# Cross-attention output stage: reciprocals spread in two bursts of four head pairs on 32-row groups of the array

## The reference

```python
qh = (q @ Wq + bq);  kh = (k @ Wk + bk);  vh = (v @ Wv + bv)      # per head, 64 wide
attn = einsum('bqhd,bkhd->hbqk', qh, kh) * mask
attn = exp(attn - max(attn)) * mask                               # one maximum over everything
attn = attn / (sum(attn, axis=-1, keepdims=True) + 1e-15)
out = einsum('hbqk,bkhd->bqhd', attn, vh) @ Wo + bo
x = out + residual
y = (x - mean(x)) / sqrt(var(x) + 1e-05) * gamma + beta
```

## Time and profile before

| | |
|---|---|
| Median of three runs | 1731.38 us |
| The profiled execution | 1729.62 us |
| Its span on the core | 1727.8 us |
| PE busy | 1666.0 us (96%) |
| DVE busy | 1157.9 us (67%) |
| ACT busy | 945.0 us (55%) |
| POOL busy | 419.0 us (24%) |
| Granted TensorE clock, mean | 0.986 |

### The profile page before, as it was taken

One profiled execution on the slowest core, in us unless ns is written; L12 is line 12 of the kernel. 1 busy time (PEld: TensorE's weight loads), 2 busy tenths in 40 slices (PEclk: granted clock), 3 DMA queues, 4 the chain that ended last, 5 costly groups with the idle time before them and its releaser, 6 DMA issues. The chain is left out here.

```text
span 1727.8 us, 31110 instructions
## 1 busy us (share of the span) xinstructions
PE 1666.0 (96%) x11011; PEld 848.1 (49%) x11012; DVE 1157.9 (67%) x2362; ACT 945.0 (55%) x1417; POOL 419.0 (24%) x519
## 2 busy tenths in 40 slices
PE   4999999999999999999995999999999999999997
PEld 4435556465464654645542444444444444444443
DVE  7665555665556655566545887878787877887774
ACT  7755555555545555455544555555564556555542
POOL 0000000000000000000000555555555555555556
PEclk8999999999999999999997999999999999999999
DMA  7455354452644526445236456655655456555621
GB/s 232 147 200 172 119 211 161 161 188 103 225 147 175 188 84 243 140 172 193 74 146 223 159 199 243 231 215 193 234 223 190 190 221 243 218 209 204 243 107 65
DMA packets 81469, 315.01 MB, mean 182 GB/s; under 512 B 5392, under 2 KB 9616, under 8 KB 71696
## 3 DMA queue, kind: packets, MB, share of 16 engines
q1 hardware_dynamic: 81424, 314.41, 49.7%
HBM read 184.37 MB, written 130.02 MB: 182 GB/s over the span
## 5 line engine op out<-in xcount | busy, mean ns | idle before, releaser
L70 PE MATMUL ps_s<-x_hi,g_hi 128*128 128x512 f16 x1024 | 389.7, 381 | 7.5 <-ACT s L509 7.4
L72 PE MATMUL ps_s<-x_hi,g_lo 128*128 128x512 f16 x1024 | 389.3, 380 | 0.0
L71 PE MATMUL ps_s<-x_lo,g_hi 128*128 128x512 f16 x1024 | 389.3, 380 | 0.0
L79 PE MATMUL ps_o<-u,p_hi 128*128 128x512 f16 x1024 | 388.4, 379 | 0.0
L80 PE MATMUL ps_o<-u,p_hi 128*128 128x512 f16 x1024 | 388.1, 379 | 0.0
L81 PE MATMUL ps_o<-u,p_lo 128*128 128x512 f16 x1024 | 388.1, 379 | 0.0
L509 ACT ACTIVATE s<-ps_s,c_bias 128x512 f32<-128x512 f32 x256 | 176.0, 688 | 309.5 <-PE ps_s L72 306.3
L631 DVE TENSOR_TENSOR score_max<-score_max,tile_max 128x1 f32<-128x1 f32 x257 | 40.8, 159 | 315.6 <-ACT s L509 313.8
L898 ACT ACTIVATE p_hi<-ps_bc 128x512 f16<-128x512 f32 x256 | 149.4, 593 | 176.9 <-DVE ps_bc L988 174.9
L1079 POOL PARTITION_ALL_REDUCE key_max<-score_max x1 | 0.4, 377 | 917.0 <-issue 917.0
L1099 POOL TENSOR_TENSOR y<-y,gamma_b 128x512 f32<-128x512 f32 x128 | 162.8, 1272 | 192.6 <-ACT y L908 192.6
(11 more groups left out here) (87 smaller groups left out, 2367.9 us busy)
## 6 DMA issues: line engine op xcount, KB each, us to landing
scores<-s SPq DMA_DIRECT2D x30, 2048.0 KB, 7.6
s<-scores SPq DMA_DIRECT2D x30, 2048.0 KB, 7.8
x<-xT_in SPq DMA_DIRECT2D x32, 1024.0 KB, 9.5
u_halves<-u_out SPq DMA_DIRECT2D x64, 512.0 KB, 3.0
u<-u_halves SPq DMA_DIRECT2D x16, 2048.0 KB, 11.8
y<-x_in SPq DMA_DIRECT2D x32, 1024.0 KB, 10.2
out<-y SPq DMA_DIRECT2D x31, 1024.0 KB, 4.2
mask<-maskT_in SPq DMA_DIRECT2D x32, 256.0 KB, 10.4
```

Source lines behind the costliest of these rows:

```text
L70: pe.matmul(out, lhs_hi, rhs_hi, start=first, stop=False)
L71: pe.matmul(out, lhs_hi, rhs_lo, start=False, stop=False)
L72: return pe.matmul(out, lhs_lo, rhs_hi, start=False, stop=last)
L79: pe.matmul(out, lhs_hi, rhs_hi, start=False, stop=False, skip_group_check=True)
```

## The change

The three product banks and four spread banks (`OBANKS` 3, `RBANKS` 4) trade places. The spreads of a unit come in two bursts, before (0,2) and before (2,0), each of eight matmuls for four pairs. Each matmul uses only the 32 rows of its own q, in weights and data, so that four matmuls in a row use four different row groups and four different banks. Each burst has two rounds of four; between them PE waits on a new semaphore, `r_halves`, which the first round's last matmul raises, since the second round writes the other half of the same banks. The sums move from before (1,7) to directly behind the second burst. Pairs are taken in the order 0, 1, 4, 5, 2, 3, 6, 7, in which both halves of four pairs cover all four q. With three banks for four tiles, the bank of a tile is the running tile number modulo 3, but for the last of a group (`o_bank`), and `fill` waits for the tile 2, 3 or 4 before (`o_since`); the first product tile of a new bank must have been read by `residual`. ACT's fills and DVE's scales, splits and residuals stand in a new order.

```diff
-SBANKS, GBANKS, OBANKS, RBANKS = 2, 4, 4, 3
+SBANKS, GBANKS, OBANKS, RBANKS = 2, 4, 3, 4
...
-        spread_at = {(0, 2): 0, (0, 5): 1, (1, 0): 2, (1, 3): 3, (1, 6): 4, (2, 1): 5, (2, 4): 6, (2, 7): 7}
-        sums_at = (1, 7)
+        spread_at = {(0, 2): 0, (2, 0): 1}
+        sums_at = (2, 0)
+        order = (0, 1, 4, 5, 2, 3, 6, 7)
+        def o_bank(u, t):
+            k = u * TB + t
+            return ps_o[1 if k == UNITS * TB - 1 else k % OBANKS]
+        def o_since(u, t):
+            return {0: 4, 1: 2, 2: 4, UNITS * TB - 1: 2}.get((u * TB + t) % (UNITS * TB), OBANKS)
...
-            def spread(n, s, p):
-                if p == 0:
+            def spread(n, s, half):
+                if half == 0:
                     pe.wait_ge(r_all_done, n + 1)
-                pe.wait_ge(p_lo_done, n * NP + (p + 1 if p >= RBANKS else (2, 3, 1)[p]))
-                for th in range(2):
-                    mm = pe.matmul(ps_bc[p % RBANKS][:, th * HT:(th + 1) * HT], sel_bc[:, p, th, :], r_all[:, s, :],
-                                   start=True, stop=True)
-                mm.then_inc(r_spread, 1)
+                pe.wait_ge(p_lo_done, n * NP + half * RBANKS + RBANKS)
+                for k in range(2):
+                    if k == 1:
+                        pe.wait_ge(r_halves, 2 * n + half + 1)
+                    for j in range(RBANKS):
+                        p, th = order[half * RBANKS + j], (j + k) % 2
+                        q = 2 * th + p // 4
+                        mm = pe.matmul(ps_bc[j][:, th * HT:(th + 1) * HT], sel_bc[32 * q:32 * q + 32, p, th, :],
+                                       r_all[32 * q:32 * q + 32, s, :], start=True, stop=True, skip_group_check=True)
+                    if k == 0:
+                        mm.then_inc(r_halves, 1)
+                mm.then_inc(r_spread, RBANKS)
...
-                    for p in range(NP):
-                        if more and (t, p) in spread_at:
-                            spread(n + 1, 1 - s, spread_at[t, p])
-                        if more2 and (t, p) == sums_at:
+                    for i, p in enumerate(order):
+                        if more and (t, i) in spread_at:
+                            spread(n + 1, 1 - s, spread_at[t, i])
+                        if more2 and (t, i) == sums_at:
                             sums(n + 2, s)
                         if t == 0:
-                            pe.wait_ge(p_lo_done, n * NP + p + 1 + RBANKS)
+                            pe.wait_ge(p_lo_done, n * NP + i + 1 + RBANKS)
                         cols = slice(t * P, (t + 1) * P)
-                        mm = add_product(pe, ps_o[t % OBANKS][:, :], (p_hi[:, s, p, cols], p_lo[:, s, p, cols]),
+                        mm = add_product(pe, o_bank(u, t)[:, :], (p_hi[:, s, p, cols], p_lo[:, s, p, cols]),
                                          (u2[:, b, place(p), 0, :], u2[:, b, place(p), 1, :]))
                     mm.then_inc(o_summed, 1)
...
-            def round_p(n, s, p):
-                if p == 0:
+            def round_p(n, s, i):
+                if i == 0:
                     act.wait_ge(o_summed, TB * n + TB)
-                act.wait_ge(p_scaled, n * NP + p + 1)
-                act.activation(p_hi[:, s, p, :], ps_bc[p % RBANKS][:, :], ACT.Copy).then_inc(p_hi_done, 1)
-            def fill(n, t):
-                act.wait_ge(y_added, n * TB + t + 1)
-                act.activation(ps_o[t % OBANKS][:, :], bo_b[:, :], ACT.Copy, scale=P_SCALE * U_SCALE).then_inc(bo_filled, 1)
+                act.wait_ge(p_scaled, n * NP + i + 1)
+                act.activation(p_hi[:, s, order[i], :], ps_bc[i % RBANKS][:, :], ACT.Copy).then_inc(p_hi_done, 1)
+            def fill(n, u, t):
+                act.wait_ge(y_added, n * TB + t + 1 + TB - o_since(u % UNITS, t))
+                act.activation(o_bank(u % UNITS, t)[:, :], bo_b[:, :], ACT.Copy, scale=P_SCALE * U_SCALE).then_inc(bo_filled, 1)
...
-                    if more:
-                        fill(n + 1, 0)
+                    if u < UNITS - 1:
+                        fill(n, u, 3)
                     norm(g, u, 0)
                     halves(4, 5)
                     if more2:
                         r_first(n + 2)
+                    if u == UNITS - 1:
+                        fill(n, u, 3)
                     if more:
-                        fill(n + 1, 1)
+                        fill(n + 1, u + 1, 0)
                     norm(g, u, 1)
                     halves(6)
                     if more2:
                         r_second(n + 2)
                     halves(7)
+                    if u < UNITS - 1:
+                        fill(n + 1, u + 1, 1)
+                    norm(g, u, 2)
+                    if u == UNITS - 1 and more:
+                        fill(n + 1, u + 1, 1)
                     if more:
-                        fill(n + 1, 2)
-                    norm(g, u, 2)
-                    if more:
-                        fill(n + 1, 3)
+                        fill(n + 1, u + 1, 2)
...
                     split(0)
                     scale(2)
                     split(1)
-                    residual(g, u, 0)
                     scale(3)
                     split(2)
+                    residual(g, u, 0)
+                    split(3)
                     shift_of(g, u, 0)
                     scale(4)
-                    split(3)
+                    scale(5)
+                    residual(g, u, 1)
+                    split(4)
                     if more2:
                         invert(n + 1)
-                    residual(g, u, 1)
-                    scale(5)
-                    split(4)
-                    shift_of(g, u, 1)
                     scale(6)
                     split(5)
+                    shift_of(g, u, 1)
                     if more2:
                         second_part(n + 1)
                     scale(7)
                     split(6)
-                    residual(g, u, 2)
                     if more2:
                         third_part(n + 1, 1 - s)
                     split(7)
+                    residual(g, u, 2)
                     shift_of(g, u, 2)
```

More of the change, by code:

```diff
@@ L726, in output_phase @@
         rest_done, r_mid_done, r_all_done = sem("rest_done"), sem("r_mid_done"), sem("r_all_done")
-        r_spread, p_scaled = sem("r_spread"), sem("p_scaled")
+        r_halves, r_spread, p_scaled = sem("r_halves"), sem("r_spread"), sem("p_scaled")
         p_hi_done, p_lo_done = sem("p_hi_done"), sem("p_lo_done")
@@ L867, in _ @@
             sums(0, 0)
-            for p in range(NP):
-                spread(0, 0, p)
+            for half in range(2):
+                spread(0, 0, half)
             sums(1, 1)
@@ L952, in _ @@
                 round_p(0, 0, p)
-                if p % 2 == 1:
-                    fill(0, p // 2)
+                if p % 2 == 1 and p < 2 * OBANKS:
+                    fill(0, 0, p // 2)
             r_first(1)
@@ L963, in _ @@
             dve.sem_inc(p_lo_done, RBANKS)
-            dve.sem_inc(y_added, OBANKS)
+            dve.sem_inc(y_added, TB)
             def invert(n):
@@ L983, in third_part, with scale_p, split_p @@
                    .then_inc(r_all_done, 1)
[L985 to L992, removed]
+            def scale_p(n, s, i):
+                dve.wait_ge(r_spread, n * NP + i + 1)
+                spread = ps_bc[i % RBANKS][:, :]
+                dve.tensor_tensor(spread, s32[:, s, order[i], :], spread, ALU.mult).then_inc(p_scaled, 1)
+            def split_p(n, s, i):
+                dve.wait_ge(p_hi_done, n * NP + i + 1)
+                p = order[i]
+                dve.tensor_tensor(p_lo[:, s, p, :], ps_bc[i % RBANKS][:, :], p_hi[:, s, p, :], ALU.subtract)\
                    .then_inc(p_lo_done, 1)
@@ L1002, in residual @@
                 y = y32[:, u, t, :]
-                dve.scalar_tensor_tensor(y, ps_o[t % OBANKS][:, :], 1 / (P_SCALE * U_SCALE), y, ALU.mult, ALU.add)\
+                dve.scalar_tensor_tensor(y, o_bank(u, t)[:, :], 1 / (P_SCALE * U_SCALE), y, ALU.mult, ALU.add)\
                    .then_inc(y_added, 1)
-                dve.wait_ge(y_added, k + 1 + OBANKS)
+                dve.wait_ge(y_added, k + 1 + TB)
                 dve.bn_stats(stats[:, t, :], y)
@@ L1063, in _ @@
             third_part(0, 0)
[L1064 to L1068, removed]
+            for half in range(2):
+                for i in range(half * RBANKS, (half + 1) * RBANKS):
+                    scale_p(0, 0, i)
+                    if i % RBANKS > 0:
+                        split_p(0, 0, i - 1)
+                split_p(0, 0, i)
             invert(1)
```

## The result

The changed kernel takes 1759.89 us in the median of four runs (1759.25 to 1760.04), against 1731.66 us for the kernel before (1730.5 to 1732.52). The ratio is 1.0165, 95% interval 1.015 to 1.0179: slower by 1.65%, 28.2 us. The profiled execution takes 1760.04 us with a span of 1758.2, 30.4 more than the span before. That is 2.2 more than between the medians, because the profiled execution of the kernel before lies 2.0 us under its median.

What follows compares the result with a forecast made beforehand. PE bounded the old kernel at 24.44 us a unit; a ring through DVE, ACT and POOL would bound the new one at 25.53. 31 x 1.09 = +33.8 us takes the median from 1731.4 to 1765.2 us, range 1747 to 1788.

Steps and rivals of the forecast that it cites:

- The ring: Closed chain of waits through DVE, ACT and POOL between successive second bursts: 25.53 us a unit instead of 24.44; chance 0.80.
- the signs: PE idle about 1.3 us before (2,0), `den` 25.5 apart, scale 0 near 5 us, granted clock still 1.0.
- The walk: Link-by-link sum over DVE's and ACT's new order, from one second burst to the next: 25.53 us.
- the price of burst 2 until DVE may start: From the second burst's start until DVE may scale: 0.91 us, bounds 0.45 and 1.6.
- The round: Four spread matmuls on four row groups, side by side on PE: 0.31 us until the result is there.
- the entry: PE's start of a burst, priced as at the sums: 0.10 us.
- PE's own unit: PE's time for a unit if nothing waits: 24.22 us, 0.22 less than before.
- the rival in which PE stays the bound: The ring closes in under 24.2 us, so PE's 24.22 decides: -7 us, 1724.5 us; chance 0.06.
- The sum: 31 units with a second burst, each 1.09 us longer: +33.8 us; prologue and last unit taken at nothing.
- The serial rival: Row groups run one after another, 1.6 us at the second burst, unit 26.2, time 1787; chance 0.10.

Runs made afterwards that it cites:

- POOL's edit: POOL makes tile 3's inverse deviation before tile 2's gamma and beta: on the changed kernel 1719.98 us (0.9939), on the kernel before 1732.83 us (1.0011).

## Why the prediction was right

The forecast was 1765.2 us, +33.8, in a range from 1747 to 1788; measured was 1759.9, +28.2. Step by step:

**The ring and its place.** PE waits before burst 2, for split 3, 1.19 us in the row's bracket and 1.27 by the units (25.23 less PE's own 23.96), against 1.3 forecast. Burst 1 waits for nothing, no product waits for a fill, DVE's idle time before `den` went, that before shift 3 is 2.76 us, and scale 0 starts right behind it, about 5 us into the unit. Two of the signs came only in part: successive `den` are 25.2 apart and not 25.5, and the granted clock did not stay at 1.0 everywhere (last section). The ring's parts were then shown one at a time: POOL's gamma and beta are in it (40 us with them out of the way), so is the place of residual 2 (30), burst 2's delay (10), and 0.2 us of the exponential.

**Its length.** The walk gave 25.53, the trace 25.23. Of the 0.30, 0.21 is the price of burst 2 until DVE may start: 0.70 measured, 0.91 taken. That is the term that was mis-sized. The round was nearly right: four matmuls on four row groups in 0.29 us, where 0.31 was worked out from the sums' column groups, 0.04 too much in two rounds. The rest is the way between and around the rounds. PE's weight loads in burst 2 of the changed kernel:

```profile
1210.67 0.10 PEld L850 LDWEIGHTS ps_bc<-r_all,sel_bc 32*128 32x128 bf16 x4 [1.68 <-DVE p_lo L1017]
1211.04 0.10 PEld L850 LDWEIGHTS ps_bc<-r_all,sel_bc 32*128 32x128 bf16 x4 [0.26 <-PE ps_bc L850]
```

The second round starts 0.37 us after the first, where the parts taken add up to 0.46 (0.31, 0.05 and 0.10). And 0.37, 0.29 and the hand-off of 0.04 already make the 0.70: the entry of 0.10, which stands ahead of burst 1 (1224.80 to 1224.89), does not show where PE has been waiting. Why it doesn't, no run shows. The other 0.1 lies in DVE's pitches between scale 4 and shift 1: after 0.70, shift 1 is due at 7.42 by the walk, and came at 7.32.

**PE's own unit.** Taken at 24.22 if nothing waits, it is 23.96, seen with the ring open. Burst 1 occupies 0.67 (0.83 taken): 0.09 for the entry, 0.37 to the second round, and 0.21 from there to the next product, where the prediction took 0.27 with 0.15 for leaving, a figure that no row stood behind. And burst 2 with the sums 2.45 + 0.10 = 2.55 (2.64 taken). Hence the rival in which PE stays the bound would have given 1731.7 - 31 x 0.48 = 1717, not 1724.5; POOL's edit gave 1720.

**What was left out.** The sum was 31 x 1.09, with nothing else in it. Measured, from the loop's first sums to the last, are 29 x 0.79 = 22.8 in the regular units, 3.2 for the loops' ends (six times 0.5, and 0.3 in the last group) and 1.5 for the clock, together 27.5. The other 2.9 of the 30.4 lie outside: 0.6 ahead of the first sums of the phase, where nothing was changed, and 2.7 in the prologue, which was taken at nothing, or up to 2 us less; the end gives 0.4 back. In the prologue PE waits for `r_all` before the loop's first burst, in the changed kernel and then in the one before:

```profile
945.29 0.65 PE L850 MATMUL ps_bc<-r_all,sel_bc 32*128 32x256 bf16 x8 [4.41 <-DVE r_all L1006]
...
946.76 0.63 PE L79 MATMUL ps_o<-u,p_hi 128*128 128x512 f16 x1
```

```profile
943.74 0.39 PE L832 MATMUL ps_bc<-r_all,sel_bc 128*128 128x256 bf16 x2 [2.92 <-DVE r_all L982]
```

The burst comes 1.0 us later within the phase. Behind it the granted clock fell to its lower level and products took 0.63 us instead of 0.38, so that PE reached burst 2 after 11.44 us, where burst 1 and 42 products at the full clock take 9.74: about 1.7 more. In the kernel before the clock stayed at 1.0 there.

So the ring gave less than forecast, 0.79 us a unit instead of 1.09, and terms that nobody forecast brought the total back to 30.4 against 33.8. That the total lies so near is in part luck. A ring that bounds pays for every irregularity of any engine in it.

**The rules.** The Trainium skill, TensorE: Matmul & The Clock Gate, Part 3, was nearer than the estimate: matmuls on different row groups run together, one matmul and a few nanoseconds long. Here four matmuls last 0.29 us (0.27 for one, as worked out in the prediction). The serial rival, with three more pitches of 0.108 in each round, is out.

```profile
1200.03 0.29 PE L850 MATMUL ps_bc<-r_all,sel_bc 32*128 32x256 bf16 x4
```

This second round of a burst 1 (the window cuts the first one off) shows the four as one row of 0.29 us. TensorEngine Tiling (Array Packing), of the Trainium skill, Theoretical Speedup, gives up to 4x for a dimension of 32, as an upper bound. This use stays far below it: PE's time for all spreads went from 1.73 us a unit to about 1.25 (1.73 less 0.48), a factor of 1.4. Of burst 1's 0.67 us the entry, the step between the rounds (0.37 less 0.29) and the way out are a good part.

## What to carry to other kernels

When small steps that were spread over a loop are gathered into bursts that need all their buffers at once, walk the whole ring from one burst to the next over every engine's written order, and put the sum beside the time of the engine that bounds. The link to shorten need not be on a busy engine: look for an instruction that is short and waited for, queued behind long ones that nobody waits for. Measure a saving with the ring open, or the saving and the new wait can't be told apart.

## What the runs showed that was not expected

After four of the six waits of 1.69 us at burst 2 (those behind a loop's end), the granted TensorE clock fell from 2.4 to 1.2 GHz; after none of the waits of 1.19 us did it. Stretches of 2 us in the changed kernel (length, busy us of PE, PEld, DVE, ACT, POOL with their instructions, granted clock, DMA share, GB/s):

```profile
1056.00:1058.00 2.00, 0.42 (x2) 0.00 (x0) 1.79 (x4) 1.82 (x3) 0.57 (x2) 1.00 1.01 391
1058.00:1060.00 2.00, 1.81 (x24) 1.00 (x28) 1.45 (x4) 1.27 (x2) 0.83 (x2) 0.73 0.19 72
1060.00:1062.00 2.00, 2.00 (x22) 0.65 (x12) 1.89 (x5) 0.74 (x2) 1.92 (x3) 0.50 0.00 0
1062.00:1064.00 2.00, 2.00 (x13) 0.88 (x10) 1.97 (x3) 0.00 (x0) 0.68 (x2) 0.91 0.00 0
```

PE ended its last product's issue at 1056.3, idled until burst 2 at 1058.11, and the clock was at 0.50, the lower level, through the sums at 1060 to 1062. They took 3.47 us instead of 1.93 (2.8 to 3.5 in the four):

```profile
1058.11 0.65 PE L850 MATMUL ps_bc<-r_all,sel_bc 32*128 32x256 bf16 x8 [1.69 <-DVE p_lo L1017]
1058.69 3.47 PE L832 MATMUL ps_sum<-s,sel_sum 128*32 128x256 f32 x32
```

The loss of up to 1.6 us is mostly covered, since PE had 1.2 us of waiting ahead of it anyway: the next unit took 25.60 instead of 25.23, 0.4 us more, 1.5 us in all four. With round 3 ahead of the exponential the six waits behind loop ends were 1.46 or 1.47 us, and no sums there took longer than 1.93. In the prologue it fell behind the waits of 4.41 us here and of 3.95 in the kernel with bursts over all 128 rows, and not behind 2.92 in the kernel before or 3.41 in the one with POOL's edit on top of those bursts. So the length of the wait alone doesn't decide. What does was not tried.

POOL's edit made the kernel before slower by 0.11% (0.02 to 0.21). The traces show the end of the program growing. The last residual of the kernel before starts at 1718.94 and its last gamma 3.75 us later; with the edit they are at 1721.16 and 5.10 us apart, because gamma and beta of the last tile but one now stand between (first the kernel before, then the edited one):

```profile
1722.69 1.26 POOL L1099 TENSOR_TENSOR y<-y,gamma_b 128x512 f32<-128x512 f32 x1 [1.17 <-ACT y L908]
```

```profile
1726.26 1.26 POOL L1099 TENSOR_TENSOR y<-y,gamma_b 128x512 f32<-128x512 f32 x1
```

These 1.35 us are most of the 1.9 us that the ratio gives.
